# Moving projections of an attention and FFN kernel into other stretches, with matmuls on ones ahead of the first

## The reference

```python
xn = layernorm(x)
q = xn @ Wq.T + bq                     # 32 heads of 16
k, v = ctx @ Wk.T + bk, ctx @ Wv.T + bv  # 8 groups of 16
w = softmax(mask(q k^T / 4))
x = x + (w v) @ Wo.T + bo
hn = layernorm(x)
h = gelu(silu(bitlinear(hn, w1, b1)))  # 2048 wide
h = layer_norm(h) * ln_g + ln_b
x = x + bitlinear(h, w2, b2)
```

## Time and profile before

| | |
|---|---|
| median of 3 runs | 582.51 us (580.14 to 583.58) |
| profiled execution, its own time | 581.34 us |
| span of the profiled execution | 579.3 us |
| mean granted clock of TensorE | 0.964 |
| TensorE, VectorE, ScalarE, GpSimd busy | 90%, 85%, 61%, 24% |

### The profile page before, as it was taken

How to read it: one execution, slowest core, us unless ns; L and a number is a source line. 1 busy time by engine, 2 the same in 40 slices (tenths; PEclk the granted TensorE clock), 3 DMA queues, 4 the chain that set the end, 5 groups by cost and what they waited for, 6 DMA issues and landing times.

```text
span 579.3 us, 9027 instructions
## 1 busy us (share of the span) xinstructions
PE 520.6 (90%) x3425; PEld 285.6 (49%) x3425; DVE 491.1 (85%) x730; ACT 351.4 (61%) x424; POOL 139.9 (24%) x106
## 2 busy tenths in 40 slices
PE   4978788999899999899999999999949999798796
PEld 3856335544564557445663566445514553243343
DVE  4689929789989788988999789978896889959996
ACT  2235470687848764785659573866368576876931
POOL 5103034003410621025200611211122105133130
PEclk9986899999899999999999999999969999988999
DMA  6888595887126712463137502571115411110002
GB/s 200 277 209 317 174 279 156 335 304 170 37 66 197 163 43 79 160 179 86 72 117 183 117 16 98 161 170 40 43 39 140 101 40 42 27 30 1 36 2 75
DMA packets 32994, 72.17 MB, mean 125 GB/s; under 512 B 7167, under 2 KB 14529, under 8 KB 29950
## 3 DMA queue, kind: packets, MB, share of 16 engines
q1 hardware_dynamic: 31286, 67.13, 39.6%
q0 software_dynamic: 576, 4.19, 1.8%
q10 hardware_dynamic: 1088, 0.24, 0.2%
HBM read 46.50 MB, written 20.61 MB: 116 GB/s over the span
## 4 chain that ended last, share of the span: by engine, by line
PE 54%; DVE 20%; issue 8%; DMA 7%; ACT 7%; POOL 2%; SPq 2%; ACTq 0%; DVEq 0%
PE FF L891 8%; PE FF L943 6%; DVE negm L1416 5%; PE S L773 5%; PE PV L813 5%; ACT PT L1136 5%; PE PV L830 4%; PE S L797 4%; PE FF L710 3%; DMA num<-o_raw 2%; PE PV L773 2%; PE FF L893 2%; DVE work L1565 2%; POOL st L510 2%; PE FF L905 2%
## 5 line engine op out<-in xcount | busy, mean ns | idle before, releaser
L1136 ACT ACTIVATE PT<-S 128x1024 f32<-128x1024 f32 x128 | 123.4, 1032 | 24.0 <-PE S L797 23.6
L1416 DVE TENSOR_REDUCE negm<-S 128x4 f32<-128x1024 f32 x88 | 105.6, 1215 | 17.9 <-PE S L773 16.5
L797 PE MATMUL S<-Q,K 100*128 100x512 bf16 x256 | 73.7, 393 | 18.6 <-ACT PT L1136 14.9
L891 PE MATMUL FF<-w1t,xqT 128*128 128x512 bf16 x256 | 68.4, 390 | 5.0 <-ACT wq_sb L1170 3.4
L813 PE MATMUL PV<-PT,vaug 128*32 128x256 f32 x1024 | 70.5, 394 | 0.6 <-ACT PT L1136 0.6
L773 PE MATMUL S<-K,Q 97*128 97x256 bf16 x352 | 55.5, 284 | 5.4 <-DVE negm L1416 3.5
L830 PE MATMUL PV<-wo_sb,num 128*128 128x512 f32 x128 | 59.1, 608 | 0.0
L1170 ACT ACTIVATE work<-FF,s 128x512 f32<-128x512 f32 x48 | 33.0, 687 | 36.3 <-PE FF L893 36.3
L1416 DVE TENSOR_REDUCE negm<-PV 128x4 f32<-128x1024 f32 x40 | 48.8, 1220 | 5.6 <-PE PV L773 5.2
L710 PE MATMUL FF<-xnT,wq_sb 128*128 128x256 f32 x224 | 50.6, 381 | 0.2 <-ACT xnT L1103 0.2
L1194 ACT ACTIVATE work<-work 128x2048 bf16<-128x2048 f32 x12 | 22.9, 1911 | 45.2 <-DVE work L1571 45.0
(11 more groups left out here) (231 smaller groups left out, 905.2 us busy)
## 6 DMA issues: line engine op xcount, KB each, us to landing
Q<-q_d SPq DMA_DIRECT2D x15, 768.0 KB
q_d<-part SPq DMA_DIRECT2D x8, 768.0 KB, 3.6
x_sb<-in_x SPq DMA_DIRECT2D x8, 512.0 KB, 4.1
ctx_sb<-in_ctxT SPq DMA_DIRECT2D x8, 512.0 KB, 4.6
work<-in_w SPq DMA_DIRECT2D x4, 1024.0 KB, 13.2
q_d<-part SPq DMA_DIRECT2D x8, 512.0 KB, 3.3
xb_sb<-in_x SPq DMA_DIRECT2D x8, 512.0 KB, 4.3
work<-in_w POOLq DMA_DIRECT2D x4, 1024.0 KB, 8.9
```

The lines of the kernel that those rows point to most:

```text
L797: last = pe.matmul(where, K[0:ROWS_2, g, kt * P:(kt + 1) * P], Q[0:ROWS_2, g, 2 * pair:2 * pair + 2, :], start=not masked, stop=True)
L891: pe.matmul(FF[:, n % 2, :], xqT[:, k, t * P:(t + 1) * P], w1t[:, k, cols], start=(k == 0), stop=False)
L1136: act.activation(PT[:, n % PT_SLOTS, :, :], ST[n % 2][:], ACT.Exp, scale=0.25).then_inc(S["pt_made"], 1)
L1416: dve.tensor_reduce(negm[:, t, R * g:R * g + R], RING_1[n % 3][:], AX.X, ALU.max, negate=True).then_inc(S["max_made"], 1)
```

## The change

V of batches 0 and 1 leaves the start: both go between the first scores of batch 0, behind n = 2 and n = 4, into the two banks of FF. The context of batch 1 goes to `xb_sb` instead of `ctx_sb` and no longer waits for V of batch 0. Ahead of K of batch 0 stand eleven matmuls on the tile of ones. ScalarE copies the V's after the first of the four weight sums.

x and Q of batch 4 leave the head of the body with `t = 0` for the tail of the body before, where the first scores of batch 2 run: `turn_x(4)` behind n = 10, the four quarters of Q behind n = 12 to 15. ScalarE copies x ahead of the first GELU, and writes Q behind the first GELU and behind the first deviations. VectorE makes the rests of Q of batch 4 right after `max_rows`, and `spread_3` and the first `gain` of batch 0 behind them.

```diff
--- before.py
+++ after.py
@@ -200,11 +200,19 @@
         def front_flat(w):
             return S0[:, :, :].rearrange("p r t -> p (r t)") if w == 1 else FFw
 
+        ctx_first = xb_sb[:].rearrange("p t n -> p (t n)").rearrange("p (k t) -> p k t", k=KD)
+
+        def ctx_of(a):
+            return ctx_first if a == 1 else ctx_sb[:, :, :]
+
+        def v_place(a):
+            return FFw[:, 512 * a:512 * a + 256] if a < 2 else FFw[:, 512:768]
+
         def x_front(a):
-            return S1[:, :, :] if a > 3 else front_of(a)
+            return S1[:, :, :] if a > 4 else front_of(a)
 
         def x_front_flat(a):
-            return S1[:, :, :].rearrange("p r t -> p (r t)") if a > 3 else front_flat(a)
+            return S1[:, :, :].rearrange("p r t -> p (r t)") if a > 4 else front_flat(a)
 
         def pair_of(a):
             return S1[:, :, :].rearrange("p r t -> p (r t)") if a < 2 else FFw
...
@@ -285,10 +293,13 @@
                 sp.dma_start(x_sb[:], x[a]).then_inc(S["x_in"], 16)
 
             def load_context(a):
-                wait_for(sp, S["kv_ps"], a)
-                sp.dma_start(ctx_sb[:], ctxT[a]).then_inc(S["ctx_in"], 16)
+                if a > 1:
+                    sp.wait_ge(S["kv_ps"], a)
+                sp.dma_start(ctx_of(a), ctxT[a]).then_inc(S["ctx_in"], 16)
 
             def load_residual(c):
+                if at_start(c):
+                    sp.wait_ge(S["kv_ps"], 2)
                 wait_for(sp, S["x1_made"], 2 * c)
                 sp.dma_start(xb_sb[:], x[c]).then_inc(S["xr_in"], 16)
 
...
@@ -683,11 +694,12 @@
                 if at_start(a):
                     pe.wait_ge(S["c_ident"], 2)
                 pe.wait_ge(S["xn_made"], 2 * a + 2)
-                if a > 3:
+                if a == 4:
+                    pe.wait_ge(S["silu_made"], 8)
+                if a > 4:
                     pe.wait_ge(S["max_made"], 16 * (a - 2) + 14)
                 if a == 2:
-                    pe.wait_ge(S["q_made"], 4)
-                    pe.wait_ge(S["r1q_made"], 4)
+                    pe.wait_ge(S["v_placed"], 2)
                 if a == 3:
                     pe.wait_ge(S["k_bo"], 1)
                 to = x_front(a)
...
@@ -728,18 +739,19 @@
                     pe.wait_ge(S["out_made"], 2 * (a - 3))
                 to = pair_of(a)
                 for k in range(KD):
-                    last = pe.matmul(to[:, 0:T], wkv_sb[:, k, 0:P], ctx_sb[:, k, :],
+                    last = pe.matmul(to[:, 0:T], wkv_sb[:, k, 0:P], ctx_of(a)[:, k, :],
                                      start=(k == 0), stop=(k == KD - 1))
                 last.then_inc(S["k_ps"], 1)
 
             def project_v(a):
-                if a == 1:
-                    pe.wait_ge(S["v_placed"], 1)
-                to = pair_of(a)
+                if a == 0:
+                    pe.wait_ge(S["q_made"], 4)
+                    pe.wait_ge(S["r1q_made"], 4)
+                to = v_place(a)
                 for t in range(TT):
                     for k in range(KD):
-                        last = pe.matmul(to[:, 512 + t * P:512 + (t + 1) * P],
-                                         ctx_sb[:, k, t * P:(t + 1) * P], wkv_sb[:, k, P:2 * P],
+                        last = pe.matmul(to[:, t * P:(t + 1) * P],
+                                         ctx_of(a)[:, k, t * P:(t + 1) * P], wkv_sb[:, k, P:2 * P],
                                          start=(k == 0), stop=(k == KD - 1))
                 last.then_inc(S["kv_ps"], 1)
 
...
@@ -753,7 +765,6 @@
                 if a == 0 and n == 1:
                     pe.wait_ge(S["k_made"], 2)
                     pe.wait_ge(S["r1k_made"], 2)
-                    pe.wait_ge(S["v_placed"], 2)
                 if n == (0 if a > 0 else 4):
                     pe.wait_ge(S["rows_in0"], 16 * ROW_LOADS * (a + 1))
                 if n == 8:
...
@@ -946,7 +957,7 @@
                     last.then_inc(S["f2_ps"], 1)
 
             def body_of(c, a, f, t, masked):
-                w = next_front(a) if c > 1 else None
+                w = next_front(a) if c > 2 else None
                 if w is not None:
                     turn_x(w)
                 if f is not None and not at_start(f):
...
@@ -992,6 +1003,11 @@
                             turn_x(3)
                         if n in (10, 12, 14, 15):
                             project_q(3, ((10, 12, 14, 15).index(n),))
+                    if at_start(f):
+                        if n == 10:
+                            turn_x(4)
+                        if n >= 12:
+                            project_q(4, (n - 12,))
                     if f is not None and n < 8:
                         layer_1(f, n, t)
                     if t is not None and n >= 8:
...
@@ -1060,6 +1076,8 @@
                 pe.wait_ge(S["c_identb"], 1)
                 for n in range(16):
                     scores_1(0, n, masked)
+                    if n in (2, 4):
+                        project_v(n // 2 - 1)
                     if n == 12:
                         turn_x(2)
                 project_q(2, (0, 1))
...
@@ -1072,15 +1090,16 @@
 
                 over_batches(body)
 
+            pe.wait_ge(S["c_ones"], 1)
+            for _ in range(11):
+                pe.matmul(PV[:, 0, 0:P], ones[:], ones[:], start=True, stop=True)
             project_k(0)
             turn_x(0)
-            project_v(0)
             project_q(0)
             mask_flag()
             turn_x(1)
             project_q(1)
             project_k(1)
-            project_v(1)
             pe.wait_ge(S["k_flagi"], 1)
             first_body(pe.value_load(flag_i[0:1, 0:1], min_val=0, max_val=1))
 
...
@@ -1237,19 +1256,20 @@
                 if at_start(a):
                     keys(0)
                     turned_x(0)
-                    values_in(0)
                     queries(0, 0)
                     queries(0, 1)
                     turned_x(1)
                     queries(1, 0)
                     queries(1, 1)
                     keys(1)
+                    weight_abs_sum(0, (0,))
+                    values_in(0)
                     values_in(1)
-                    weight_abs_sum(0, (0, 1, 2))
+                    weight_abs_sum(0, (1, 2))
                     turned_x(2)
                     weight_abs_sum(0, (3,))
                     return
-                w = next_front(a) if c != 1 else None
+                w = next_front(a) if c not in (1, 2) else None
                 if w is not None and c > 0:
                     turned_x(w)
                 if t is not None:
...
@@ -1280,9 +1300,15 @@
                 if f is not None:
                     for n in range(8):
                         silu(f, n)
+                    if at_start(f):
+                        turned_x(4)
                     gelu(f, 0)
+                    if at_start(f):
+                        queries(4, 0)
                     gelu(f, 1)
                     deviations(f, 0)
+                    if at_start(f):
+                        queries(4, 1)
                     deviations(f, 1)
 
             over_batches(body)
...
@@ -1765,7 +1791,7 @@
                 w = next_front(a)
                 if c is not None:
                     maximum_parts(c)
-                if t is not None:
+                if t is not None and not at_start(t):
                     spread_3(t)
                     gain(t, 0)
                 if at_start(c):
...
@@ -1774,8 +1800,11 @@
                     max_rows(c)
                 if at_start(c):
                     weight_scale(0)
-                if at_start(f):
+                if at_start(f) or at_start(t):
                     query_rests(w)
+                if at_start(t):
+                    spread_3(t)
+                    gain(t, 0)
                 if t is not None:
                     shift(t, 0)
                 if f is not None:
...
@@ -1785,7 +1814,7 @@
                     shift(t, 1)
                 if at_start(c):
                     quantise_weight(0, w1t[:].rearrange("p k n -> p (k n)"))
-                if w is not None and not at_start(f):
+                if w is not None and not at_start(f) and not at_start(t):
                     query_rests(w)
                 if t is not None:
                     maximum_2(t, 0)
```

More of the change, by code:

```diff
@@ L1128, in values_in @@
                 act.copy(vaug[:, a % 2, :, :, 0:HD],
-                         pair_of(a)[:, 512:512 + TT * P].rearrange("p (t g d) -> p t g d", t=TT, g=G)
+                         v_place(a).rearrange("p (t g d) -> p t g d", t=TT, g=G)
                          ).then_inc(S["v_placed"], 1)
```

## The result

The changed kernel takes 588.81 us (median of 4 runs, 587.67 to 591.65) against 582.19 (580.14 to 583.58) for the kernel before beside it: a ratio of 1.0114, 95% interval 1.0076 to 1.0151. It is slower by 6.6 us; the forecast was 586.5 in 582.5 to 590. The profiled execution is the longest of the four, 591.65 us with a span of 589.7, which is 10.4 more than the span before; the medians are 6.6 apart. Where this one execution lost 3.5 us more will be seen at the start; the other three have no trace.

What follows compares the result with a forecast made beforehand. Whichever queue arrives last at each hand-over was taken as the bound, not one engine's share. Start -2.05, first exp +5.15 and slow clock +1.5 gave +4.6: 585.9 profiled, 586.5 median, range 582.5 to 590.

Steps and rivals of the forecast that it cites:

- the tail: First scores of batch 2, now with x and Q of batch 4: last maximum ends at 160.7, 1.6 late.
- the head: Start of batch 2's second scores: second shift ends at 179.3 instead of 172.05, first exp +5.15.
- the pause and its clock: TensorE idles from 172.5 to 184.7, then one half-clock stretch costs +1.5, bounds 0 and 3.
- the table load: Exp table load ahead of batch 2's exps: charged 1.28 a switch, without the skill's extra drain of 1.38.
- rival E: Table switch at batch 2's exps: the skill page's drain is paid, sum +6.0, 588; chance 0.03.
- Sum of the start: -2.05: From kernel start to first row maximum: ones and moved V's save 2.05 us, bounds -2.5 and 0.
- K ends at 9.9: K of batch 0 behind the ones: if the clock is still up after the idling, 1.89 us are saved.
- forecast first maximum 33.6: End of the start's chain: first row maximum near 33.6 instead of 35.70.
- the added 0.6: Step from profiled execution, 585.9, to median, 586.5: half of the 1.2 by which the median lay above it.
- B: Head of batch 2's second scores: projections were the bound, first exp at 172.3, 6.2 earlier, 574; chance 0.10.
- C: TensorE's pause costs nothing and the start gives its most: +2.65, 584.5 to 585; chance 0.21.
- D: Clock falls before K of batch 0, ones buy nothing, start gains 0 to 0.4: +6.5, 588.5; chance 0.18.

Runs made afterwards that it cites:

- Experiment 1: Kernel before with only x and Q of batch 4 moved, with ScalarE's and VectorE's orders for it, start untouched: 591.38 us, ratio 1.0140.
- experiment 5: Changed kernel with VectorE's old order (spread and gain filling the wait, rests of Q behind the shifts) and ScalarE's deviations ahead of its Q copies: 584.97 us.
- experiment 6: Experiment 5 with only four bank-emptying rests ahead of the shifts, roundings later, second residual earlier, second squares behind exp n = 1, Q stored later: 581.09 us.
- experiment 2: Changed kernel with batch 4's part taken back, so only the start is changed (eleven ones, V's moved): 581.98 us, ratio 0.9996.
- experiment 4: Changed kernel with ScalarE making batch 0's two squares behind exps n = 2 and n = 7 instead of ahead of all exps: 592.69 us, ratio 1.0173.
- experiment 8: Experiment 2 plus twelve filler matmuls of 512 bf16 columns ahead of batch 1's first scores: 581.64 us, ratio 0.9981.
- experiment 3: Experiment 2 without the eleven matmuls on ones, V's still moved: 581.66 us, ratio 0.9991.
- experiment 10: Experiment 2 with 24 ones in place of 11 and the twelve filler matmuls ahead of batch 1's first scores: 581.63 us, ratio 0.9982.
- experiment 7: Experiment 2 with 24 matmuls on ones in place of 11: 581.05 us, ratio 0.9956.
- experiment 9: Experiment 6 with 24 ones in place of 11 and twelve filler matmuls ahead of batch 1's first scores: 579.89 us, ratio 0.9955.

## Why the prediction was right, and where it was not

**Right: the tail.** An end of the last maximum 1.6 us late was forecast; from the projection of batch 0 to there it is 52.84 us after (164.29 - 111.45) against 51.13 before, 1.7 late.

**Right: the head.** The second shift was to end 18.6 us behind the last maximum (179.3 - 160.7); it ends 18.48 behind (182.77 - 164.29), where it was 12.94 before. The first exp moves from 178.53 to 186.84; less the 3.47 us inherited from the start that is +4.84, forecast +5.15. Experiment 1 shows that this edit makes the loss. Experiments 5 and 6 keep the projections where the change puts them and give 584.97 and 581.09, so the loss lies in the orders built around them and not in the move itself: VectorE's, whose second shift the exps wait for, and with it ScalarE's, whose late deviations would have held back `spread_3` in the old order as well. The two were given back together; how much each is worth alone is open.

**Right: the pause and its clock.** TensorE idles 11.78 us and the clock is 0.50 from 180 to 192. First scores of batch 3 come 10.04 us late; less 3.47 and 4.84, 1.73 belong to the slow stretch, forecast 1.5. Head, tail and clock are 6.57, and the medians differ by 6.6. The closeness of these two is partly luck: 6.57 is read from one pair of executions and leaves their start out, and experiment 1, with the same head and the old start, lost 8.8.

**Right: the table load.** The exp call stands at 186.12, at the end of the load (184.83 + 1.28), although ScalarE is now last at this hand-over. The drain of 1.38 us that the Trainium skill (ScalarE: Activation LUTs, "What ACT_TABLE_LOAD costs") adds to a switch of set does not show here either; rival E was nothing.

**Wrong: the term "Sum of the start: -2.05".** Two steps of it failed. The first is that the clock would still be up, so that K ends at 9.9: K took 3.23 us. That step is not a certainty in either direction. With eleven ones it ran at half clock for the most part in the profiled executions of the kernel after and of experiments 2, 4 and 5 (3.23 to 3.67), behind 2.26 to 2.59 us of idling, and at full clock in 6 and 8 (1.99), behind 1.75 and 1.85. The idling was shorter there because the same 22 passes took 5.06 us, 6 or 7 in each microsecond to the end, against 4.18 to 4.67: where the ones never got fast, K did, and where they got fast, it did not. Where it ran full the rest of the step was right: forecast first maximum 33.6, measured 33.54. The second failure is larger: what was worked out for the first maximum was carried on to the end of the kernel. In the medians of experiments 2, 3, 8 and 10 between 0.6 and 1.6 us of 582 are left of it, none clear of the noise, and 2.2 in experiment 7; in the pair of traces 3.47 us of loss stand in its place. The next wait behind it, for the rows of batch 1 at 85, was in the trace of before (1.21 us at 85.03) and I did not follow the gain so far. Why the rows land when they do I can only argue: the scores that need them started between 83.74 and 86.88 in all twelve profiles, in no clear order with TensorE's arrival, and in all of them the DMA share is 0.91 to 1.15 from 76 to 84. No experiment took transfers away.

**The size.** The sum was +4.6 for the profiled execution, 585.9, and the forecast added 0.6 because the median stood 1.2 above it before. The profiled execution after took 591.65 instead: 10.3 more, of which 3.47, 4.84 and 1.73 are named above. The median stood 2.8 below it, so the added 0.6 has no ground. That 588.81 lies within 582.5 to 590 rests on head, tail and pause, which were right, and on a range wide enough for a start that gave nothing.

**The rivals.** B, 574, fell as its own condition said: the second shift ended at 182.77, not before 168.3. C needed no price for the pause, and it had one. D was half right: K ran at half clock for the most part in the profiled execution, and the median came 0.3 from its 588.5, since a start worth nothing makes the sum +6.6. But its reason is not the whole one: in experiment 7 K took 1.89, and the profiled execution still took 582.85, with nothing of the 2.05 left.

## What to carry to other kernels

Taking work off the engine that comes last at a hand-over is worth at most the distance to the second engine, and only if that engine's queue is not made longer for it: here 8.9 us off TensorE cost 6.6, because the rests of Q were put ahead of a gain and two shifts on which ScalarE waited. Where a moved product needs an operation early, split that operation's consumers and move only what frees the bank. Follow a gain at the start to the next wait on a transfer before it enters the sum, and where a full engine will arrive early there, price the clock that it loses in the pause.

## What was not expected of the hardware

A pause of two to four microseconds can cost more than its length. At the handover TensorE idled 3.33 to 4.14 us in the kernel after and experiments 1, 4, 6 and 7, and 2.13 and 2.16 us in 5 and 3. In each the granted clock then stood at 0.50: in five of them already in the pause or as it ended, in 3 and 5 about 1 us behind it, so that the first eight matmuls still took 1.05 instead of 1.89. In all but 4 it fell once more near 98. From handover to projection it was 25.1 to 26.5 us in these (23.9 in 4), and 22.95 and 22.79 in the kernel before and experiment 2, which idled 1.21 and 0.38 us and kept their clock. Twelve matmuls on whatever was at hand, 2.76 us of them, kept the clock at 1.00 through the handover, and it still fell to 0.50 near 96, for 23.8 us in all.

It is tempting to say that one slow stretch spares the next, since in the kernel before TensorE came late enough out of the first to find the rows nearly there. Experiments 3, 4 and 5 do not bear that out: they had a clock of 0.72, 0.72 and 0.75 from 66 to 72, like the kernel before, and fell at the handover all the same.

The same work ahead of K is also not the same length from one execution to the next: 24 matmuls on ones took 7.35, 8.06 and 8.45 us in experiments 7, 9 and 10. Counted in windows of one microsecond, 6 or 7 of their passes end in each at first and 10 to 12 later, and the change comes near 5, 6 and 7 us. The granted clock of the profile does not show it: it reads 1.00 in all of these windows, as it does from 8 to 12 in the kernel before, where K took 3.78 us. Before the first fall that it records, the durations are the safer reading.
